# Which middle tables of a recommendation tower are looked up in sums, and which engine sums them

## The reference, cut to what matters

```python
e = stack([tbl_f[ids[:, f]] for f in range(39)], axis=1)      # [2048, 39, 64]
s = sum(e, axis=-1)                                           # [2048, 39]
z = s[:, ROW] * s[:, COL]                                     # all 741 pairs
h = relu(concat([z, dense_ctx]) @ W_top1 + b_top1)            # 757 -> 512
h = relu(h @ W_top2 + b_top2)                                 # 512 -> 256
y = h @ W_top3                                                # [2048, 1]
```

## Time and profile before

| | |
|---|---|
| median of 3 runs | 198.97 us (198.95 to 199.9) |
| profiled execution | 199.26 us |
| its span, first to last instruction | 197.5 us |
| mean granted TensorE clock | 0.965 of full |
| PE, DVE, POOL, ACT busy | 173.5, 127.0, 136.4, 81.2 us |
| moved by DMA | 40.64 MB |

### The profile page before, as it was taken

One profiled execution on the slowest core, in us unless ns is written; L12 is line 12 of the kernel. 1 busy time (PEld: TensorE's weight loads), 2 busy tenths in 40 slices (PEclk: granted clock), 3 DMA queues, 4 the chain that ended last, 5 costly groups with the idle time before them and its releaser, 6 DMA issues.

```text
span 197.5 us, 4456 instructions
## 1 busy us (share of the span) xinstructions
PE 173.5 (88%) x1735; PEld 112.3 (57%) x1735; DVE 127.0 (64%) x328; ACT 81.2 (41%) x145; POOL 136.4 (69%) x140
## 2 busy tenths in 40 slices
PE   0598998768998799999578999999989899999993
PEld 0133543222786377666445767687756468767682
DVE  1611864687924864865858988987768977645440
ACT  0579798789001913415202320641141334233323
POOL 6777777778777777777877777877777777771000
PEclk9999999965599999999999999999999999999999
DMA  5998799999516935999999999111951111111000
GB/s 196 415 333 225 248 339 406 389 393 392 185 27 197 406 128 161 404 341 330 211 354 394 388 390 361 51 23 37 242 97 22 27 27 32 23 24 13 0 3 0
DMA packets 14549, 40.64 MB, mean 206 GB/s; under 512 B 3184, under 2 KB 5632, under 8 KB 14400
## 3 DMA queue, kind: packets, MB, share of 16 engines
q1 hardware_dynamic: 9872, 35.60, 50.4%
q0 software_dynamic: 4224, 4.33, 9.6%
q10 hardware_dynamic: 432, 0.42, 0.8%
HBM read 40.07 MB, written 0.27 MB: 204 GB/s over the span
## 4 chain that ended last, share of the span: by engine, by line
POOL 53%; PE 23%; issue 16%; DMA 4%; DVE 1%; ACT 1%; DVEq 0%
POOL rows L395 35%; POOL rows L404 18%; PE ph L1137 4%; PE ph L1141 4%; PE ph L1138 4%; DMA rows<-tab,idc 3%; PE ph L1157 2%; PE ph L1161 2%; PE ph L1158 2%; DMA idc<-ids_cols 2%; PE s L1116 1%; PE g L1076 1%; PE g L1051 1%; PE ph L1169 1%; DVE picked L509 0%
## 5 line engine op out<-in xcount | busy, mean ns | idle before, releaser
L395 POOL DMA_INDIRECT rows<-tab,idc x84 | 85.4, 1017 | 26.7 <-issue 25.3
L404 POOL DMA_INDIRECT rows<-tab,idc x48 | 48.8, 1017 | 14.6 <-issue 14.6
L1137 PE MATMUL ph<-z_hi,w_hi 126*128 126x512 f32 (+1 forms) x96 | 42.8, 446 | 0.5 <-ACT z_hi L839 0.4
L1141 PE MATMUL ph<-z_lo,w_hi 126*128 126x512 f32 (+1 forms) x96 | 39.3, 409 | 1.2 <-DVE z_lo L565 1.2
L1138 PE MATMUL ph<-z_hi,w_lo 126*128 126x512 f32 (+1 forms) x96 | 38.9, 405 | 0.0
L488 DVE TENSOR_SCALAR hots<-hots,fc 125x2048 bf16<-125x2048 bf16 x28 | 21.2, 771 | 14.8 <-ACT hots L788 14.0
L509 DVE SCALAR_TENSOR_TENSOR picked<-slot_b,fc,g 128x512 bf16<-128x512 bf16 x28 | 20.2, 742 | 7.1 <-PE g L1051 6.8
L1137 PEld LDWEIGHTS ph<-z_hi,w_hi 126*128 126x128 f32 (+1 forms) x96 | 18.9, 197 | 7.0 <-issue 3.3
L1141 PEld LDWEIGHTS ph<-z_lo,w_hi 126*128 126x128 f32 (+1 forms) x96 | 18.7, 195 | 7.4 <-DVE z_lo L565 3.2
L839 ACT CAST z_hi<-z 126x512 fp32r<-126x512 f32 (+1 forms) x24 | 14.7, 622 | 18.4 <-DVE z L559 18.3
L559 DVE TENSOR_TENSOR z<-factors,s 126x512 f32<-126x512 f32 (+1 forms) x24 | 15.9, 683 | 9.5 <-PE s L1116 6.6
(11 more groups left out here) (83 smaller groups left out, 225.7 us busy)
## 6 DMA issues: line engine op xcount, KB each, us to landing
stage<-middle SPq DMA_DIRECT2D x12, 800.0 KB, 10.0
hots<-shelf_scratch SPq DMA_DIRECT2D x17, 512.0 KB, 14.2
stage<-middle SPq DMA_DIRECT2D x4, 750.0 KB
stage<-early SPq DMA_DIRECT2D x3, 768.0 KB, 6.2
rows<-tab,idc POOLq DMA_INDIRECT x132, 3.9
stage<-early SPq DMA_DIRECT2D x3, 640.0 KB, 6.8
slot_b<-slot_scratch SPq DMA_DIRECT2D x8, 224.0 KB, 8.1
stage<-early SPq DMA_DIRECT2D x3, 512.0 KB, 3.9
```

What stands on the lines that cost most here:

```text
L395: pool.indirect_dma_start(rows[:, n % ROW_RING, i, :], None, gathered[i], bass.IndirectOffsetOnAxis(ap=idc[:, n, i:i + 1], axis=0)).then_i ...
L404: pool.indirect_dma_start(rows[:, n % ROW_RING, i, :], None, gathered[i], bass.IndirectOffsetOnAxis(ap=idc[:, n, i:i + 1], axis=0)).then_i ...
L1137: pe.matmul(ph[m][:, :], hi, z_hi[0:n, zi, :], start=(k == 0), stop=False)
L1141: mm = pe.matmul(ph[m][:, :], hi, z_lo[0:n, zi, :], start=False, stop=(k == KCH - 1))
```

## The change

Chunk 0 looks up one middle table, chunk 1 four, chunks 2 and 3 five. Tables 1 and 3 are paired and summed by PE as before. Tables 0, 2 and 4 (`ROW_SUMMED`) lie in DRAM a shelf to a row, [125, 6400] floats, are loaded a shelf to a partition, and DVE sums each quarter in two instructions. The slots of chunk 0 are copied out of PSUM by DVE, not ACT. All lists have a new order; the diff shows SP's and the parts of the others that the prediction speaks of.

```diff
-SUMMED = (0, 3, 4, 4)
+SUMMED = (1, 4, 5, 5)
+ROW_SUMMED = (0, 2, 4)
+SLOT_COLS = WMID // PIECES
+SLOT_HALVES = [(0, 13), (13, SLOT_COLS)]
...
             def load_middle(m, q):
                 if m == 0:
                     sp.wait_ge(table_summed, (len(BATCHES) - 1) * PIECES + q + 1)
+                elif m - 1 in ROW_SUMMED:
+                    sp.wait_ge(rows_summed, 2 * (ROW_SUMMED.index(m - 1) * PIECES + q + 1))
                 else:
-                    sp.wait_ge(mid_summed, (m - 1) * PIECES + q + 1)
+                    sp.wait_ge(mid_summed, PAIR_SUMMED.index(m - 1) * PIECES + q + 1)
                 a, e = q * STAGE_COLS, min((q + 1) * STAGE_COLS, mid_tabs[m].shape[1])
-                sp.dma_start(stage[:, q, 0:e - a], mid_tabs[m][:, a:e]).then_inc(stage_in[q], 16)
+                sp.dma_start(stage[0:mid_tabs[m].shape[0], q, 0:e - a], mid_tabs[m][:, a:e]).then_inc(stage_in[q], 16)
...
             load_middle(2, 3)
+            load_middle(3, 0)
+            load_middle(3, 1)
+            load_middle(3, 2)
+            load_middle(3, 3)
             load_shelves(2, 0)
...
             load_shelves(2, 3)
-            load_slots(2)
             load_shelves(2, 4)
             load_shelves(2, 5)
             load_shelves(2, 6)
-            load_middle(3, 0)
-            load_middle(3, 1)
-            load_middle(3, 2)
-            load_middle(3, 3)
+            load_middle(4, 0)
+            load_middle(4, 1)
+            load_middle(4, 2)
+            load_middle(4, 3)
+            load_slots(2)
             load_mid_shelves(2)
...
+            def row_sum(m, q, x):
+                n = ROW_SUMMED.index(m)
+                a, e = SLOT_HALVES[x]
+                dve.wait_ge(stage_in[q], 16 * (len(BATCHES) + m + 1))
+                dve.tensor_reduce(mid_sums[0:SHELVES, n, q * SLOT_COLS + a:q * SLOT_COLS + e],
+                                  stage[0:SHELVES, q, a * DIM:e * DIM].rearrange("p (w d) -> p w d", d=DIM), AX.X,
+                                  ALU.add).then_inc(rows_summed, 1)
+            def split_rows(m):
...
+            def slot_copy(c, g, bank):
+                dve.wait_ge(slot_spread, c * GROUPS + g + 1)
+                dve.tensor_copy(slot_b[:, g, :], bank[:, :]).then_inc(slot0_copied, 1)
...
-    mid_tabs = [dram(f"middle_{m}", paired([MIDDLE[m]])) for m in range(NMID)]
+    mid_tabs = [dram(f"middle_{m}", table(MIDDLE[m]).reshape(SHELVES, -1) if m in ROW_SUMMED else paired([MIDDLE[m]]))
+                for m in range(NMID)]
```

More of the change, by code:

```diff
@@ L37 @@
 ORDER = EARLY + MIDDLE + LARGE
-SUMMED = (0, 3, 4, 4)
+SUMMED = (1, 4, 5, 5)
 NMID = max(SUMMED)
+ROW_SUMMED = (0, 2, 4)
+PAIR_SUMMED = tuple(m for m in range(NMID) if m not in ROW_SUMMED)
 LANE = 32
@@ L246, in mid_picks, with mid_loads @@
             return sum(SUMMED[:c]) * TILES + t * SUMMED[c] + a
+        def mid_loads(c):
+            return 16 * sum(1 + (SUMMED[x] > 4) for x in range(2, c + 1))
         def rows_a(c):
@@ L597, in _ @@
[L597 to L603, removed]
+            row_sum(0, 3, 1)
             multiply(0, 0)
             multiply(0, 1)
-            multiply(0, 2)
+            hot(1, 2)
             z_low(0, 0)
-            pick(1, 0, G0)
+            sum_b(0, 0)
             z_low(0, 1)
[L610 to L622, removed]
+            split_rows(0)
+            pick(1, 0, G1)
+            mid_hot(0)
             hot(1, 3)
-            z_low(0, 3)
             hot(1, 4)
@@ L627, in _ @@
             hot(1, 6)
[L628 to L635 removed]
+            mid_pick(0, 0, 0, 1, G0, 1)
+            mid_pick(0, 1, 0, 1, G1, 2)
+            sum_b(0, 1)
+            multiply(0, 2)
+            sum_a(0, 3)
+            dve.wait_ge(mid_picked_ready, 1)
+            mid_pick(0, 2, 0, 1, G0, 3)
+            z_low(0, 2)
@@ new lines, in _ @@
+            sum_b(0, 2)
+            split_w1(3)
+            split_w1(4)
+            split_w1(5)
+            dve.wait_ge(mid_picked_ready, 2)
+            mid_pick(0, 3, 0, 1, G0, 4)
+            split_mid(1, G1)
+            split_a(0)
+            sum_b(0, 3)
+            row_sum(2, 0, 0)
+            pick(1, 1, G0)
+            split_b(0)
+            row_sum(2, 0, 1)
+            row_sum(2, 1, 0)
+            multiply(0, 3)
+            pick(1, 2, G1)
+            sum_a(1, 0)
+            multiply(0, 4)
@@ L636, in _ @@
+            z_low(0, 3)
+            multiply(0, 5)
+            row_sum(2, 1, 1)
+            mid_hot(1)
+            pick(1, 3, G1)
+            sum_a(1, 1)
+            row_sum(2, 2, 0)
+            z_low(0, 4)
+            z_low(0, 5)
+            pick(1, 4, G1)
+            row_sum(2, 2, 1)
+            pick(1, 5, G0)
+            sum_a(1, 2)
+            pick(1, 6, G1)
+            row_sum(2, 3, 0)
+            row_sum(2, 3, 1)
             h1_low(0, 0)
-            sum_a(1, 1)
+            split_rows(2)
@@ L681, in _ @@
+            multiply(1, 3)
+            sum_a(2, 0)
+            multiply(1, 4)
+            z_low(1, 3)
+            multiply(1, 5)
+            z_low(1, 4)
+            sum_a(2, 1)
+            z_low(1, 5)
+            pick(2, 0, G0)
+            pick(2, 1, G1)
+            mid_hot(2)
+            pick(2, 2, G0)
+            hot(3, 0)
             pick(2, 3, G1)
             pick(2, 4, G0)
-            mid_hot(2)
-            z_low(1, 5)
-            hot(2, 6)
-            sum_a(2, 0)
-            sum_a(2, 1)
@@ L688, in _ @@
-            pick(2, 5, G0)
-            hot(3, 0)
-            hot(3, 1)
-            split_mid(3, G1)
-            pick(2, 6, G0)
+            row_sum(4, 1, 1)
+            row_sum(4, 2, 0)
+            row_sum(4, 2, 1)
             h1_low(1, 0)
             h1_low(1, 1)
+            pick(2, 5, G1)
+            pick(2, 6, G0)
             h1_low(1, 2)
+            row_sum(4, 3, 0)
+            row_sum(4, 3, 1)
+            sum_b(2, 0)
+            split_rows(4)
             h1_low(1, 3)
-            hot(3, 2)
+            multiply(2, 0)
@@ L715, in _ @@
             split_a(2)
+            sum_b(2, 2)
+            sum_b(2, 3)
+            hot(3, 1)
+            split_b(2)
+            sum_a(3, 0)
+            multiply(2, 3)
+            hot(3, 2)
+            hot(3, 3)
+            z_low(2, 3)
             hot(3, 4)
-            sum_b(2, 0)
-            sum_b(2, 1)
-            sum_b(2, 2)
+            multiply(2, 4)
+            hot(3, 5)
+            sum_a(3, 1)
+            z_low(2, 4)
             mid_hot(3)
-            hot(3, 5)
-            multiply(2, 3)
```

776 lines of the change are left out of this document (397 added, 379 removed).

## The result

The changed kernel takes **257.28 us** (median of 4 runs, 255.3 to 258.59) where the kernel before takes 198.96 (4 runs, 197.81 to 199.9): ratio 1.2926, 95% interval 1.2817 to 1.3036. The forecast was 230 with a range of 198 to 242. The direction was right and the size was not: 58 us were lost and 31 foreseen. The profiled execution took 255.3 us for a span of 253.5, its mean granted clock 0.865.

What follows compares the result with a forecast made beforehand. Gathers on POOL pace the first 145 us, PE's queue the last 50, DMA close by. Serial five-engine loads put h1_low(1,0) at 154; 154 + 75.4 = 229.4, + 1.8 - 0.3, rounded down to 230 us; range 198 to 242.

Steps and rivals of the forecast that it cites:

- the price of a 125-row load: Row-table loads: 125 rows dealt evenly to five engines, 25 rows each at 24.4 GB/s, 6.56 us a load, 26.2 a table.
- rival B: Row-table loads: a different five engines for each load, so quarters run beside each other; 197 us, no change; chance 7%.
- The signs named: Trace: row-table loads 6 us or more, DVE waiting before first z, z at 60 or later, picks waiting until about 145.
- last gather: POOL: sixteen gathers fewer take off 21.1 us, so its last one ends at 157.2, PE's end 70 us behind.
- rival A: Row-table loads dealt to all sixteen engines, 2.1 us each; span 186.5, time 188 us; chance 9%.
- Step 1: Early tables summed sooner; the last weight load lands at 33 us, where it was 40.6 before.
- Step 2: Table 0 takes 26.2 us, to 59.2; DVE's row sums hold the first product until 61, late by 16 us.
- Step 3: Three shelf loads, table 1, then table 2 loaded by 98.7; chunk 0's end about 22 us late.
- Step 4: Tables 3 and 4, then chunk 2's slots at 145 behind table 4; picks wait, h1_low(1,0) at about 154.
- Step 5: From h1_low(1,0) to the end: PE's 73.2 us before, with additions 75.4, ending at 229.4.
- Rival C: Five engines in order, plus PE restarting at half clock, 3.7 us twice, the second counting: 234 us; inside the 84%.
- slower engines beside the gathers: Upper end of the range: DMA engines slowed by gathers, together with PE's half-clock restart, add up to 12 us.

Runs made afterwards that it cites:

- before_split_c: Kernel before, its sixteen middle-table quarter loads each sent as 125 rows and 3 rows, nothing else changed: 275.75 us, ratio 1.386.
- rows128_again: Changed kernel with its three row tables padded with zero rows to 128 rows: 199.76 us, ratio 0.9976 to the kernel before.
- rows127: Changed kernel with its row tables padded to 127 rows, a prime: 547.01 us, one run.
- short_sums_b: Changed kernel padded to 128 rows, row sums of 64 elements each, on 330 to 333 us chips: 0.9528, 0.9554, 0.9626 in three sets.

## Why the prediction missed

**The failed step is the price of a 125-row load, 6.56 us; the mechanism was right.** A row table took 31.4 to 32.7 us and not 26.2, and three of them on the path make 18 of the 24 us by which the span was missed (253.5 against 229.4). Five engines of 25 rows, the same five each time, in turn: quarters of table 0 landed one after another, never beside each other, which excludes rival B; 128 rows undid it, which excludes rival A for the kernel as written. The signs named were there: DVE waiting for stage ahead of the first z, z past 60, picks waiting for slot_b, PE's end 72 us behind the last gather. One was not: that last gather came at 181.8 and not near 157.

**Step 1, the weights: 33 forecast, 37.9 measured** (issued at 26.07, landed 11.8 later). The forecast used 390 GB/s with hardly a gap (by its own bytes, 11.0 MB, that is 28.2 us, not 29). 5 us.

**Step 2, table 0: 26.2 us forecast, 31.4 measured** (37.9 to about 69.3), and its price is the term that failed. I costed a 125-row load at the rate an engine has in a full, even stretch. It has that rate when its four fellows work alone (6.35 us in before_split_c); while the other eleven carry shelves, and then table 1's first quarters, a quarter took 9.5. The order of service was as forecast, shelf loads behind the table on the five engines. 5 us, and with step 1 the first z stood at 71.77, not 61.

**Step 3, table 2: 98.7 forecast, 113.86 measured.** Its first quarter was issued at 81.20, 8.7 us later than the 72.5 forecast, and the table took 32.7 us instead of 26.2, again by slow quarters (6.5 us). Table 1 between them cost what was forecast.

**Step 4, slots: 145 forecast, 169.23 measured.** Nine more than step 3 passed on, and the packet records part them. Table 4's 500 packets went from 130.6 to 163.3, 32.7 us instead of 26.2, which is 6.5 us (it began 1 us earlier than step 3's delay would have it). The slots on the five engines followed from 163 to 169, some 6 us where 2.4 were forecast. SP's stall in its four slot issues was not in the forecast at all, but it is not why the slots were late: the eleven other engines moved their part of each slot load, 154 packets, as soon as it was issued, and the last issue ended at 152.7, 10 us before table 4 was through. What SP issues after the slots, the stall does delay. Then `h1_low(1,0)` at 179.22: 10.0 behind the pick, 9 forecast.

**Step 5, the tail: 75.4 forecast, 253.5 - 179.2 = 74.3 measured.** Right to 1 us. Rival C's restart was there, ahead of this step: PE worked at half clock from 170.0 to 175 (granted clock 0.50, then 0.98 from 175 to 180), within the 10.0 us of step 4, so it is at most a small part of the miss. In all, 229.4 + 15.2 (steps 1 to 3) + 9.0 + 1.0 - 1.1 = 253.5, the span of the profiled execution. That execution is the shortest of the four, 2 us below the median.

**GpSimd: last gather at 157.2 forecast, 181.8 measured.** Wrong for a reason I had not looked for: gathers of chunk 1 wait for the last of `w_lo`, which stand in the new DVE list behind table 0's row sums, and so GpSimd stood 28.2 us (5.0 in rows128_again, 122.7 in rows127). It is off the path here (the chain that ended last has no GpSimd in it), but it took back all 21 us.

**Rival A was also wrong, by 12 us.** With mended loads the span is 198.8 against its 186.5. The last gather of chunk 1 ended at 97.8, not 93.4 (the 5.0 us wait for `w_lo`); turn_b followed 9.9 us later, not 6.1; from there to the end 91.2 us, not 87.0. A fuller DVE, whose slices stand at 8 or 9 over most of 40 to 105 us, would fit all three; no experiment settled it.

**The range was too narrow.** Its upper end allowed 12 us for "slower engines beside the gathers" and the clock together. Twelve loads, most of them in series, each with an uncertain price, should have had a wide end of their own: at the 9.5 us measured beside busy engines it would have been 12 x 2.9 = 35 us.

## What to carry to other kernels

Before a load's shape is changed, factor its row count: here a load of 125 rows took three to four and a half times as long as one of 128 (6.35 to 9.5 us against 2.1), one of 127 fifteen times, and three rows of padding took the loss back. Where a transfer sits on few engines, everything issued after it waits there with its share, the issuing engine can be held too, and the rate of a full, even stretch is the best case of its price. And look for producers (here `w_lo`) that stand behind a new wait in the same engine's list: gain taken off one engine comes back as a wait there.

## Not expected of the hardware

- All sixteen engines busy with uneven loads carried 217 GB/s at a share of 0.96, against 390 at 1.02 with even ones. Why is open.
- SP was held in the issue of loads that queue behind 125-row ones: up to 6.1 us for one that otherwise takes 0.45, and over 30 us in rows127. One slot issue of rows128_again took 4.6 us, so few engines are not the only way to it.
- One DMA engine alone moved 127 rows of 6400 bytes in 31.0 us, 26 GB/s, a little more than each of sixteen together (24.4).
- Some chips take 333 us for the kernel that takes 199 on others, with PE idle (34.7 us in front of one group in short_sums_b) where the profile shows no wait. Why is open.
